# A fused attention and gated MLP block on one core: key tiles 0 and 1 summed on VectorE, places of the maxima and banks of the projection chunks alternating by unit, first maximum drawn into the unit in front

## The reference

```python
xn = layernorm(x)
xq = rope(xn @ Wq); xk = rope(xn @ Wk); xv = xn @ Wv       # Wq 128x1024, Wk and Wv 128x512
xk = repeat(xk, 2, axis=-1); xv = repeat(xv, 2, axis=-1)   # 16 heads of 64
scores = softmax(xq @ xk.T * 0.5, axis=-1)                 # (4, 16, 1024, 1024)
attn = (scores @ xv) @ Wo
h = silu(xn @ w_gate.T) * (xn @ w_up.T)                    # int weights / 127, hidden 384
out = x + attn + h @ w_down.T
```

## Time and profile before

| | us |
|---|---|
| median of 3 runs | 1159.65 |
| lowest, highest | 1156.83, 1164.91 |
| profiled execution | 1166.15 |
| its span | 1164.4 |
| busy in the span: TensorE, VectorE, GpSimd, ScalarE | 1120.0, 901.1, 852.9, 729.8 |
| granted TensorE clock, mean | 0.984 |

### The profile page before, as it was taken

One profiled execution on the slowest core, in us unless ns is written; L12 is line 12 of the kernel. 1 busy time (PEld: TensorE's weight loads), 2 busy tenths in 40 slices (PEclk: granted clock), 3 DMA queues, 4 the chain that ended last, 5 costly groups with the idle time before them and its releaser, 6 DMA issues.

```text
span 1164.4 us, 17086 instructions
## 1 busy us (share of the span) xinstructions
PE 1120.0 (96%) x6288; PEld 663.2 (57%) x6288; DVE 901.1 (77%) x1023; ACT 729.8 (63%) x1327; POOL 852.9 (73%) x268
## 2 busy tenths in 40 slices
PE   5899899999999999999999999999999999999997
PEld 4787455655565555556565555555555555554443
DVE  7686877787887877788787877778787877776655
ACT  3234666666676666666676666666676666665564
POOL 3222868788788778888788778887778878887660
PEclk9899999999999999999999999999999999998889
DMA  6662908062340718062341718072341618050000
GB/s 230 159 258 77 256 2 224 1 205 58 85 141 19 207 37 224 2 205 57 96 129 26 201 37 224 1 210 53 96 130 30 196 37 224 1 130 1 5 1 19
DMA packets 56338, 124.98 MB, mean 107 GB/s; under 512 B 8000, under 2 KB 19520, under 8 KB 54080
## 3 DMA queue, kind: packets, MB, share of 16 engines
q1 hardware_dynamic: 56256, 123.90, 36.8%
HBM read 53.08 MB, written 10.49 MB: 55 GB/s over the span
## 4 chain that ended last, share of the span: by engine, by line
PE 79%; DVE 14%; SPq 2%; ACT 2%; issue 1%; DMA 1%; POOL 0%; DVEq 0%; ACTq 0%; POOLq 0%
PE bank_o L406 20%; PE bank_s L554 18%; PE scores L391 17%; DVE row_max L946 12%; PE scores L373 7%; PE bank_m L381 3%; PE bank_m L442 2%; PE bank_m L416 2%; PE bank_m L419 2%; SPq L239 2%; PE scores L492 2%; PE bank_s L509 1%; ACT prob L867 1%; PE bank_o L509 1%; DVE stats L961 1%
## 5 line engine op out<-in xcount | busy, mean ns | idle before, releaser
L946 DVE TENSOR_REDUCE row_max<-scores 128x1 f32<-128x1024 f32 x512 | 597.1, 1214 | 206.8 <-PE scores L391 206.5
L867 ACT ACTIVATE prob<-bank_s 128x512 f32<-128x512 f32 x992 | 576.7, 600 | 252.9 <-PE bank_s L554 229.5
L1181 POOL TENSOR_TENSOR prob_sum<-prob_sum,prob 128x2048 f32<-128x2048 f32 x93 | 425.7, 4577 | 13.5 <-ACT prob L867 0.5
L554 PE MATMUL bank_s<-qk_pack 98*128 98x512 f32 x992 | 415.8, 434 | 7.1 <-ACT prob L867 3.1
L391 PE MATMUL scores<-qk_pack 96*128 96x512 f32 x1024 | 337.5, 411 | 8.9 <-DVE row_max L946 0.3
L554 PEld LDWEIGHTS bank_s<-qk_pack 98*128 98x128 f32 x992 | 186.9, 189 | 184.9 <-issue 84.7
L406 PE MATMUL bank_o<-prob,v 128*32 128x512 f32 x2048 | 253.0, 612 | 0.0
L391 PEld LDWEIGHTS scores<-qk_pack 96*128 96x128 f32 x1024 | 179.5, 190 | 74.5 <-DVE row_max L946 53.0
L1181 POOL TENSOR_TENSOR prob_sum<-prob_sum,prob_pair 128x2048 f32<-128x2048 f32 x31 | 142.7, 4602 | 101.7 <-DVE prob_pair L1039 101.7
L1125 POOL TENSOR_TENSOR qk_stage<-rope,qk_stage 128x512 fp32r<-128x512 f32 x64 | 81.8, 1279 | 92.3 <-ACT qk_stage L753 92.3
L1173 POOL TENSOR_TENSOR prob_sum<-prob 128x2048 f32<-128x2048 f32 x31 | 142.2, 4586 | 0.0
(11 more groups left out here) (105 smaller groups left out, 742.4 us busy)
## 6 DMA issues: line engine op xcount, KB each, us to landing
qk_pack<-qk_stage SPq DMA_DIRECT2D x384, 128.0 KB, 5.0
table<-tables SPq DMA_DIRECT2D x16, 2048.0 KB, 9.6
w_stage<-w_scratch SPq DMA_DIRECT2D x14, 640.0 KB, 4.5
v<-v_stage SPq DMA_DIRECT2D x32, 256.0 KB, 8.1
xT_scratch<-xT_hl SPq DMA_DIRECT2D x4, 1024.0 KB, 9.5
x_stage<-xT_scratch SPq DMA_DIRECT2D x4, 1024.0 KB, 7.0
w_scratch<-w_split SPq DMA_DIRECT2D x1, 2560.0 KB, 15.1
x_all<-x SPq DMA_DIRECT2D x4, 512.0 KB, 11.7
```

The costliest lines, as they stand in the source:

```text
L554: mm(bank_s[:, h % 2, :], qk_pack[j][0:SCORE_K, 1, kt // QT, h, (kt % QT) * 128:(kt % QT + 1) * 128], qk_pack[j][0:SCORE_K, 0, t, h, :], s ...
L867: A(prob[:, kt % RING, h, :], bank_s[:, h % 2, :], ACT.Exp).then_inc(prob_ready, 1)
L946: V.tensor_reduce(row_max[:, m:m + 1], scores[:, at:at + 2, :].rearrange("p c k -> p (c k)"), axis=AX.X, op=ALU.max).then_inc(max_read, 1)
L1181: TT(prob_sum[:, t], prob_sum[:, t], part, ALU.add).then_inc(sum_done, 1)
```

## The change

- VectorE adds key tiles 0 and 1 of the unit straight into `prob_sum`, behind the reduction of maximum 5 (`PAIR_AFTER`); GpSimd adds key tiles 2, 3, 4, 5 and 6 to it. `prob_pair` is gone. The waits of ScalarE for free places in the ring follow.
- The place of a maximum and the bank of a projection chunk depend on the parity of the unit (`max_place`, `chunk_bank`). Maxima 0 and 1 have the same place.
- Maximum 0 of unit u+2 is computed and reduced at the end of slot u, ahead of the second half of `rotate`.
- The second half of V's projection moves behind the first score of the next slot. Key tile 0 keeps two maxima, key tile 1 has one, key tile 3 three; the other key tiles keep theirs.
- The maxima are transposed as they are; the split into rounded part and rest is done behind the transpose, by ScalarE (`high_max`) and VectorE (`low_max`), with a DMA for each.
- The inversion comes behind reduction 8 (`INVERT_AFTER`), and rounding and the read of `y` have other places in ScalarE's order.

```diff
-INVERT_AFTER = 9
+INVERT_AFTER = 8
+PAIR_AFTER = 5
...
+        def max_place(v, m):
+            return (v + (1 if m >= 2 and m % 2 == 0 else 0)) % 2
+        def chunk_bank(w, c):
+            return c if w < 4 else 2 * ((w + c // 2) % 2) + c % 2
...
-                sp.wait_ge(maxT_read, v + 1)
-                sp.dma_start(qk_pack[n][SPLIT_K:SCORE_K, 0, t].bitcast(F32).rearrange("r h q -> r (h q)"),
-                             max_rows[:]).then_inc(max_packed, 16)
+                for r, ready in enumerate((max_hi, max_lo)):
+                    sp.wait_ge(ready, v + 1)
+                    sp.dma_start(qk_pack[n][SPLIT_K + r:SPLIT_K + r + 1, 0, t].bitcast(F32).rearrange("r h q -> r (h q)"),
+                                 max_rows[r][:]).then_inc(max_packed, 16)
...
-                    last = mm(scores[:, c, :], w_from[:, a, c, :], x_from[:, r, cols], start=n == 0, stop=n == 2)
+                    last = mm(scores[:, chunk_bank(w, c), :], w_from[:, a, c, :], x_from[:, r, cols], start=n == 0, stop=n == 2)
...
-            def max_tile(v, m, n, t, places=2):
-                at_least(pe, max_read, TILES * v + m + 1 - places)
+            def max_tile(v, m, n, t):
+                at_least(pe, max_read, TILES * v + (m if v == 0 else max(m - 1, m == 1)))
+                at = 0 if v == 0 else 2 * max_place(v, m)
                 h = m // QT
                 for c in range(2):
-                    last = mm(scores[:, 2 * (m % places) + c, :], qk_pack[n][0:SPLIT_K, 0, t, h, (m % QT) * 128:(m % QT + 1) * 128],
+                    last = mm(scores[:, at + c, :], qk_pack[n][0:SPLIT_K, 0, t, h, (m % QT) * 128:(m % QT + 1) * 128],
                               qk_pack[n][0:SPLIT_K, 1, c, h, :], start=True, stop=True)
                 last.then_inc(max_ready, 1)
             def transpose_max(v):
-                pe.wait_ge(max_lo, v + 1)
-                nc.tensor.transpose(bank_m[0:2 * TILES, 0:128], max_hl[:].rearrange("p a m -> p (a m)"), ident[:]).then_inc(maxT_ready, 1)
+                pe.wait_ge(max_read, TILES * v + TILES)
+                at_least(pe, max_lo, v)
+                nc.tensor.transpose(bank_m[0:TILES, 0:128], row_max[:], ident[:]).then_inc(maxT_ready, 1)
...
-                def maxima():
-                    if do_max:
-                        m = next(tiles)
-                        if m < 2:
-                            pe.wait_ge(rope_done, capped(2 * u + 7 + m, 2 * UNITS))
+                def maxima(v=v, v_n=v_n, v_t=v_t):
+                    if v < UNITS:
+                        m = next(tiles[v])
+                        if m in (0, 2):
+                            pe.wait_ge(rope_done, capped(2 * v + 5 + (1 if m == 2 or v == 1 else 0), 2 * UNITS))
                         max_tile(v, m, v_n, v_t)
...
+                def project_half(u, t, s, n):
+                    if u + 4 < UNITS:
+                        pe.wait_ge(max_lo, u + 2)
+                        project_v(u + 4, t, blocks=range(n * QT // 2, (n + 1) * QT // 2))
...
-                if do_max and t == 1:
-                    pe.wait_ge(packed, 16 * PACKS * (s + 1))
                 for kt in range(KT):
                     score(kt, 0)
                     if kt == 0:
-                        maxima()
+                        if is_first(u):
+                            maxima()
+                        else:
+                            project_half(u - 1, 1 - t, s, 1)
                         score(kt, 1)
                         maxima()
                         score(kt, 2)
                         if not is_second(u):
                             project_out(u - 2, 1 - j, s - 1)
                         score(kt, 2)
-                        maxima()
                         score(kt, 3)
                     elif kt == 2:
                         maxima()
                         score(kt, 2)
                         maxima()
                         score(kt, 3)
+                        maxima()
                     elif kt == 4:
                         maxima()
                         score(kt, 1)
                     elif kt == 6:
                         pv_pair(kt)
                         score(kt, 1)
+                        at_least(pe, o_done, u)
+                        transpose_max(v)
                         project_chunk(0)
                         score(kt, 2)
-                        if do_max:
-                            at_least(pe, o_done, u)
-                            transpose_max(v)
                         project_chunk(1)
                         score(kt, 3)
+                    else:
                         project_chunk(2)
-                    else:
+                        score(kt, 1)
                         project_chunk(3)
-                        score(kt, 1)
-                        if not last_pair:
-                            pe.wait_ge(maxT_read, v + 1)
-                            project_v(w, t, blocks=range(QT // 2))
                         score(kt, 2)
-                        if not last_pair:
-                            project_v(w, t, blocks=range(QT // 2, QT))
+                        project_half(u, t, s, 0)
                         score(kt, 3)
+                        if t == 0 and v + 1 < UNITS:
+                            pe.wait_ge(packed, 16 * PACKS * (s + 1))
+                        maxima(v + 1, 1 - j, t)
...
+            def high_max(v):
                 act.wait_ge(maxT_ready, v + 1)
-                at_least(act, max_packed, 16 * v)
-                nc.scalar.copy(max_rows[:], bank_m[0:2 * TILES, 0:128]).then_inc(maxT_read, 1)
+                at_least(act, max_packed, 32 * v)
+                nc.scalar.copy(max_rows[0][:].bitcast(F32R), bank_m[0:TILES, 0:128]).then_inc(max_hi, 1)
...
-                        if kt < 2:
-                            act.wait_ge(pair_done, u)
-                        elif kt == 2:
-                            act.wait_ge(sum_done, 5 * u)
+                        if kt < 3:
+                            act.wait_ge(sum_done, 5 * u + kt - 2)
                         elif kt == 3:
                             act.wait_ge(den_ready, u)
                         elif kt < 6:
-                            act.wait_ge(sum_done, 5 * u + 1)
+                            act.wait_ge(pair_done, u + 1)
                         else:
-                            act.wait_ge(sum_done, 5 * u + kt - 4)
+                            act.wait_ge(sum_done, 5 * u + kt - 5)
                     for h in range(HG):
                         act.wait_ge(score_ready, 32 * u + 4 * kt + h + 1)
                         A(prob[:, kt % RING, h, :], bank_s[:, h % 2, :], ACT.Exp).then_inc(prob_ready, 1)
-                        if (kt, h) == (0, 2) and not first and staged:
-                            stage_v(u + 3, 1 - t, s + 1 + t)
+                        if (kt, h) == (0, 2) and staged:
+                            if not first:
+                                stage_v(u + 3, 1 - t, s + 1 + t)
+                            round_hi(0, u + 3, 1 - t, s + 1 + t)
                         elif (kt, h) == (0, 3) and not first:
                             read_o(u - 1)
                         elif (kt, h) == (1, 1) and staged:
-                            round_hi(0, u + 3, 1 - t, s + 1 + t)
-                        elif (kt, h) == (1, 3) and not is_second(u):
-                            read_y(u - 2)
+                            round_hi(1, u + 3, 1 - t, s + 1 + t)
                         elif (kt, h) == (2, 1):
-                            if staged:
-                                round_hi(1, u + 3, 1 - t, s + 1 + t)
+                            if not is_second(u):
+                                read_y(u - 2)
                             if not first:
                                 read_den(u - 1)
                         elif (kt, h) == (4, 1) and not first:
                             spread_inv(u - 1)
-                        elif (kt, h) == (6, 2) and not (last_pair and j == 1 and t == 1):
-                            read_maxT(u + 1)
+                        elif (kt, h) == (6, 1):
+                            high_max(u + 1)
...
+            def low_max(v):
                 dve.wait_ge(max_hi, v + 1)
-                V.tensor_tensor(max_hl[:, 1, :], row_max[:], max_hl[:, 0, :], ALU.subtract).then_inc(max_lo, 1)
+                at_least(dve, max_packed, 32 * v)
+                V.tensor_tensor(max_rows[1][:], bank_m[0:TILES, 0:128], max_rows[0][:], ALU.subtract).then_inc(max_lo, 1)
...
-            def pair_sum(u):
-                dve.wait_ge(prob_ready, NE * (KT * u + 6))
-                at_least(dve, sum_done, 5 * u - 1)
-                V.tensor_tensor(prob_pair[:], prob[:, 4 % RING], prob[:, 5 % RING], ALU.add).then_inc(pair_done, 1)
+            def pair_sum(u, t):
+                dve.wait_ge(prob_ready, NE * (KT * u + 2))
+                at_least(dve, den_ready, u - 1)
```

(86 more changed lines are left out.)

15 lines of the change are left out of this document (5 added, 10 removed).

## The result

The changed kernel takes 1204.0 us (median of 4 runs, 1201.47 to 1204.25) against 1158.95 (median of 4, 1156.83 to 1164.91): a ratio of 1.038, with an interval of 1.034 to 1.042. It is 45 us slower.

A forecast was written before the change was run, and what follows sets the result against it. TensorE was taken as the bound, in lock-step with VectorE's reductions over two PSUM places. Per slot 1.30 - 0.05 + 0.25 = 1.5 us, times 27, plus 1.0 and 3.9, gave 45.4 us and a forecast of 1205 us, range 1190 to 1219.

The forecast's parts named there:

- The stretch: From denominators to key tile 4's PV pair: six maxima instead of five, paced by VectorE's reductions; 1.30 us a slot more.
- The pair sum: VectorE's addition of key tiles 0 and 1, placed in its 2.99 us gap: costs nothing; uncovered, up to 2.28 us a slot.
- Key tiles 0 and 1: First to second PV pair of a slot: one maximum fewer, but scores wait for ScalarE; -0.05 us, bounds -0.5 and +0.3.
- The slot's end: Key tile 6's PV pair to the next slot's first: reordered work, maximum 1 waits for maximum 0's place; +0.25 us.
- The slot: One pass of the main loop, 32.7 us before: 1.5 us longer, with bounds of 1.0 to 1.9.
- The start: Slot 1, beginning when the V copy lands: maximum 0 and half of V now stand behind that landing; +1.0 us.
- The last slots: The last three slots, without projections: only the part from denominators to PV pair grows; 3.9 us together.
- The sum: Whole kernel: 40.5 us for 27 slots, 1.0 for slot 1 and 3.9 for the last three, together 45.4 us.
- the smaller loss: Rival: three successive scores cost nothing and the slot's end gains 0.2; 0.6 us a slot, 1178 us; chance 0.13.
- The granted clock: Rival: TensorE's clock falls from 2.4 to 1.2 GHz behind new waits; 1.47 us a slot more, 1249 us; chance 0.06.
- The faster rival: VectorE's relief at the slot's tail removes TensorE's waits for it, 1.7 us a slot; 1109 us; chance 0.08.
- the rival of no change: The reduction queue recovers elsewhere, taking the 1.3 us from the 3 us VectorE waited; chance 0.05.

The follow-up runs named there:

- e3: Kernel before the change, with only the second maximum of key tile 1 moved behind the last score of key tile 3: 1187.68 us, ratio 1.0216.
- e2: Changed kernel with only the inversion put back behind reduction 9: 1199.08 us, ratio 1.0313 to the kernel before.
- e1: Changed kernel with two maxima each in key tiles 1 and 3 again, pair sum behind reduction 6, inversion behind 9: 1172.13 us, ratio 1.0082.
- e4: Changed kernel with the pair sum behind reduction 7 instead of 5, out of VectorE's gap: 1324.22 us, ratio 1.1391 to the kernel before.
- e5: Kernel of e1 with the second half of the rotation put ahead of the reduction of maximum 0: 1169.04 us, one run.
- e6: Kernel of e5 with the places of the maxima strictly in turn, so maxima 0 and 1 share none: 1154.01 us, ratio 0.9931 to the kernel before.
- e7: Kernel before the change, with one maximum moved from key tile 1 to between PV pair and denominators: 1166.74 us, ratio 1.0038.

## Why the prediction was right, point by point

**The stretch** was the step that carried the forecast, and it held: +1.30 expected, +1.19 measured, of which e3 gives 1.07 for the maximum and e2 0.12 for the inversion. The maximum was put at 1.16 and measured 1.07: the reductions lie 1.13 us apart, and from the last maximum to the PV pair it takes 0.90 in e3 instead of 0.96 (520.86 to 521.82 before), where a weight load of a score had waited 0.24 for ScalarE. The inversion was reckoned at about 0.1 from its rows and entered the sum with 0.15.

**The pair sum at nothing** held (e1), with 0.36 us to spare where 0.6 was reckoned, and e4 shows its price without cover. Here the text was too low: up to 2.28 us a slot was said, 3.94 came, since the clock wasn't counted.

**GpSimd** at nothing held. Its five sums start 12.7 us into the slot and end 2.3 us into the next one (532.89 to 556.38), where 15 and 4 were reckoned.

**Key tiles 0 and 1**: -0.05 expected, -0.17 measured. That ScalarE would take back most of the maximum's 0.47 was right.

**The slot's end**: +0.25 expected, +0.23 measured, and this agreement is luck. The wait was the one named, and e5 and e6 separate it from the half rotation and the half of V, but the shared place costs 0.45, and a gain of 0.2 from the new order, which I had not seen, hides the rest.

**Key tiles 4 to 6**: 0 and 0.

**The slot**: +1.5 expected, +1.22 measured from median to median and 1.16 on the mean of 27. The bounds given for the three parts add up to 0.5 to 2.2 us; the 1.0 to 1.9 in the sum is narrower, and its working isn't given.

**The start** was mis-sized: +1.0 expected for slot 1, 2.8 measured, and the mechanism was another. I had slot 0 end ahead of the V copy's landing. The changed kernel's slot 0 is too long for that:

```profile
121.00 3.64 PE L416 MATMUL bank_o<-prob,v 128*32 128x512 f32 x16
```

This first PV pair starts 2.1 us later than before (118.89). It takes 3.64 us and not 1.92, and the extra maximum of key tile 3 puts another 1.1 between it and the next pair (10.21 us against 7.34 in all). In exchange TensorE doesn't wait for the V copy any more, which had cost it 2.45 us. Ahead of the pair TensorE waits 1.09 us for maximum 0's place, and the granted clock falls; but e1 has the same wait, and its clock stays. The windows of 116 to 121 us, of the changed kernel (granted clock 0.69) and of e1 (1.00):

```profile
116.00:121.00 5.00, 4.29 (x11) 2.33 (x10) 2.71 (x3) 3.66 (x7) 2.23 (x2) 0.69 0.96 282
...
116.00:121.00 5.00, 4.51 (x24) 2.34 (x27) 4.54 (x5) 3.75 (x7) 2.34 (x2) 1.00 0.93 275
```

So the wait alone doesn't explain the clock, and what does is not shown.

**The last slots**: +3.9 expected, +1.1 measured. The stretch grows in them too (10.24 to 10.28), 3.6 us in the three. But in the kernel before the first PV pairs of slots 29, 30 and 31 run at a low clock and take 3.39, 3.64 and 3.64 us; in the changed kernel they take 2.76, 2.88 and 1.92, which is 3.1 us less.

**The sum** was 45.4 us, and the profiled executions differ by 35.3: 31.2 in the 27 slots where I had 40.5. So the mechanism was right and its size 10 us too high. That the median came out at 1204 against 1205 is luck: the 45.4 us, 10 too many, were added to a base of 1159.65, which is 4 us under the median of the 18 later executions of the kernel before and 6.5 under the one profiled.

**The rivals**: the smaller loss had the right direction for its parts (-0.17 in key tile 1) but not enough of it. The granted clock stayed at 1.00 in mid-run (windows 520 to 554, 600 to 634 and 800 to 834). The rule of the Trainium skill, page "TensorE: Matmul & The Clock Gate", section "A second HAM failure mode: psum-queue depth-cycling", by which short idle moments between groups of matmuls make the clock swing, is not what this trace shows for waits of up to 0.7 us in the changed kernel's mid-run; e4, with one wait of 2.35 us a slot, does show the swing. The faster rival fell on the spacing of the reductions, and with it the rival of no change, as the stretch is 1.19 us longer.

## What to carry to other kernels

Where two engines alternate through two places, count the items between the points at which the slower one has run dry: each item more costs the slower engine's full time for it (1.07 to 1.13 us here), whatever the averages of busy time say. Taking one out need not give as much back (0.63 us in e7), because another engine can be next. Small work that is put among them (an inversion of 0.16 us) adds its own. A long operation belongs into the gap where that engine waits anyway. And when an item is drawn forward over a boundary, look at whose place it takes and who comes next for the same place.

## What the runs showed of the hardware

One wait of TensorE of 2.35 us in a slot was enough for the granted clock to fall to 0.58 in the window that follows, and a PV pair went from 1.92 to 3.29 us (e4); waits of up to 0.7 us, several a slot, left it at 1.00 in the changed kernel.

The pair sum takes 2.28 us in e4, where GpSimd is idle, and 2.54 us in the changed kernel, where it starts at 529.03 while an addition of GpSimd is still running:

```profile
528.14 1.27 POOL L1195 TENSOR_TENSOR y_acc<-y_part,y_acc 128x512 f32<-128x512 f32 x1 [1.65 <-ACT y_part L859]
```

They overlap by 0.38 us and the sum is 0.26 longer. The changed kernel's own trace has the comparison without that addition: in slots 0 and 1 no output of an earlier unit is there to be added, GpSimd is idle, and the sum in the same place takes 2.28 us.

```profile
156.45 2.28 DVE L1050 TENSOR_TENSOR prob_sum<-prob 128x2048 f32<-128x2048 f32 x1
```

In the other 29 slots the overlap is 0.38 to 0.40 us and the sum takes 2.54. In e1 it takes 2.53 with 0.38 us of overlap and 2.56 with 0.41, so each hundredth of overlap adds a hundredth. So it is GpSimd's addition that lengthens the sum. This fits the Trainium skill, page "SBUF — State Buffer", section "SBUF: two separate sides", by which a VectorE operation with two SBUF inputs and a GpSimd operation shut each other out of a shared port pair. The runs don't isolate the port, so that part of the cause is not shown.
